# A two-layer graph network on one core: the setup, the first and the last pairs written out in an order of their own on each engine

## The reference

```python
# layer 0
h = relu(layernorm(x))
x = x + adj @ (h @ W0) + b0
# layer 1, 8 heads of 256 features
h = relu(layernorm(x))
f = (h @ fc_w + fc_b)                       # per head: feat_proj, 128 x 256
q, k = f @ q_w + q_b, f @ k_w + k_b
masked = leaky_relu(q + k^T + (1 - adj) * -1e9, 0.01)
attn = softmax(masked)
x = x + sigmoid(concat_heads(attn @ f) @ fp_w + fp_b + h)
```

## Time and profile before

| | |
|---|---|
| median of 3 runs | 1457.86 us (1457.38 to 1458.21) |
| profiled execution, its own time | 1458.05 us |
| its span (first to last instruction) | 1456.3 us |
| PE busy | 1437.4 us, 99% |
| DVE busy | 1280.5 us, 88% |
| ACT busy | 1130.4 us, 78% |
| POOL busy | 1100.7 us, 76% |
| mean granted TensorE clock | 0.993 of 2.4 GHz |
| PE's share of the chain that ended last | 97% |

### The profile page before, as it was taken

How to read it: one execution, slowest core, us unless ns; L and a number is a source line. 1 busy time by engine, 2 the same in 40 slices (tenths; PEclk the granted TensorE clock), 3 DMA queues, 4 the chain that set the end, 5 groups by cost and what they waited for, 6 DMA issues and landing times.

```text
span 1456.3 us, 31565 instructions
## 1 busy us (share of the span) xinstructions
PE 1437.4 (99%) x9128; PEld 1286.0 (88%) x9128; DVE 1280.5 (88%) x4393; ACT 1130.4 (78%) x3477; POOL 1100.7 (76%) x1293
## 2 busy tenths in 40 slices
PE   7899999999999999999999999999999999999998
PEld 6788898898888888888988988888888988988887
DVE  5789889889889889889898898898898898898886
ACT  3677877877877878778778778778778778778776
POOL 3677777787787787787777877777777777877864
PEclk9899999999999999999999999999999999999999
DMA  5221221221221221221221221222212212212211
GB/s 191 88 103 69 87 103 60 93 102 53 100 102 52 101 102 52 101 102 52 101 94 59 101 87 67 101 79 73 102 69 84 102 59 94 102 52 101 73 47 42
DMA packets 42651, 123.88 MB, mean 85 GB/s; under 512 B 4224, under 2 KB 9216, under 8 KB 42624
## 3 DMA queue, kind: packets, MB, share of 16 engines
q1 hardware_dynamic: 42336, 123.55, 23.3%
q10 hardware_dynamic: 288, 0.01, 0.0%
HBM read 105.46 MB, written 18.09 MB: 85 GB/s over the span
## 4 chain that ended last, share of the span: by engine, by line
PE 97%; issue 1%; DMA 0%; DVE 0%; ACT 0%; POOL 0%; POOLq 0%; SPq 0%
PE gbank L272 49%; PE ybank L272 25%; PE tbank L388 8%; PE bank L272 6%; PE bank L339 4%; PE bank L367 2%; PE bank L357 2%; PE gbank L292 1%; PE bank L373 0%; DMA late<-fp_w_dram 0%; POOL att L900 0%; ACT att L750 0%; DVE kq_sb L568 0%; POOLq L44 0%; ACT h L719 0%
## 5 line engine op out<-in xcount | busy, mean ns | idle before, releaser
L893 POOL TENSOR_TENSOR att<-late,t_pos 128x512 f32<-128x512 f32 x256 | 331.1, 1294 | 135.3 <-PE tbank L388 134.2
L272 PE MATMUL gbank<-m_hi,hT_lo 128*128 128x512 f32 x1024 | 431.4, 421 | 0.0
L750 ACT ACTIVATE att<-att 128x128 f32<-128x128 f32 x1024 | 397.9, 393 | 39.8 <-DVE att L601 34.8
L272 PE MATMUL gbank<-m_hi,hT_hi 128*128 128x512 f32 x1024 | 406.1, 397 | 0.0
L272 PE MATMUL gbank<-m_lo,hT_hi 128*128 128x512 f32 x1024 | 405.7, 396 | 0.0
L577 DVE TENSOR_TENSOR g_lo<-gbank,g_hi 128x512 fp32r<-128x512 f32 x512 | 342.5, 680 | 48.0 <-ACT g_hi L743 43.1
L900 POOL TENSOR_TENSOR att<-att,rinv 128x512 f32<-128x512 f32 x256 | 289.9, 1132 | 112.4 <-DVE rinv L606 112.2
L743 ACT ACTIVATE g_hi<-gbank 128x512 fp32r<-128x512 f32 x512 | 289.9, 594 | 59.0 <-PE gbank L272 58.9
L594 DVE TENSOR_SCALAR_CACHE_REDUCE att<-att,qs 128x128 f32<-128x128 f32 x1024 | 291.9, 342 | 37.5 <-POOL att L893 37.5
L272 PE MATMUL ybank<-g_hi,pT_lo 128*128 128x256 f32 x1024 | 293.8, 287 | 0.0
L272 PE MATMUL ybank<-g_hi,pT_hi 128*128 128x256 f32 x1024 | 289.7, 283 | 0.0
(11 more groups left out here) (87 smaller groups left out, 2359.0 us busy)
## 6 DMA issues: line engine op xcount, KB each, us to landing
late<-key_rows SPq DMA_DIRECT2D x64, 1024.0 KB, 5.9
g_in<-graph_dram SPq DMA_DIRECT2D x64, 512.0 KB, 3.3
out_dram<-res SPq DMA_DIRECT2D x64, 256.0 KB, 3.2
late<-fp_w_dram SPq DMA_DIRECT2D x4, 512.0 KB, 9.2
key_rows<-kq_sb SPq DMA_DIRECT2D x64, 20.0 KB
att<-fc_wT_dram SPq DMA_DIRECT2D x2, 512.0 KB, 6.5
late<-fc_wT_dram SPq DMA_DIRECT2D x2, 512.0 KB, 9.9
w_f<-w_dram SPq DMA_DIRECT2D x1, 256.0 KB, 8.3
```

What stands on the lines that cost most here:

```text
L272: mm = pe.matmul(out_ap, w, m, start=first and n == 0, stop=last and n == len(terms) - 1)
L750: e = act.activation(a[:, s], a[:, s], ACT.Exp, scale=-1.0, bias=a[:, CH + h:CH + h + 1], accum_out=esum[j][c][:, h:h + 1])
L893: gp.tensor_tensor(a, keys[q][:, j, c * HC:(c + 1) * HC, :], t_pos[q][:, j, :].unsqueeze(1).broadcast_to([P, HC, P]), ALU.add)\
```

## The change

Nothing is computed in another way. Steps 4 to 60 of PE (and the like stretches of the other engines) keep their loop and its order. `setup` and the steps ahead of the loop become one list for each engine (`begin`), and those behind it another (`finish`), each with calls from several pairs mixed in a new order. The main points:

- The weights come in five pieces, of 1, 1, 2, 2 and 2 heads, so the first two are 0.5 MB. `load` of pair 1 is issued ahead of piece 2 and that of pair 2 ahead of piece 4. The small loads have a semaphore each instead of a shared one.
- `warm` has 10 products instead of 18.
- Pair 1's `aggregate` and `transform` stand among or right behind the folds, pair 2's and 3's between pair 0's projections; seven projections of pair 0 stand ahead of its first `transpose_p` (four before).
- `keys_queries` of pair 1 stands on DVE ahead of pair 0's `mask_min`.
- `transpose_h` waits also for `v_hTlo` of the pair before, in the loop too.
- In the last pairs the calls of `step` stand in a slightly different order.

The core of the diff (in `finish` of PE the calls go on in this manner down to `attend(63, 1, 1)`):

```diff
+WARM = 10
+
+PIECES = ((0, 1), (1, 2), (2, 4), (4, 6), (6, 8))
+STARTS = [h for h, _ in PIECES]
...
+            def weights_in(c):
+                t = slice(DT * PIECES[c][0], DT * PIECES[c][1])
+                at = slice(t.start % H, t.start % H + t.stop - t.start)
+                sp.dma_start(fcT_sb[t.start // H][:, at, :], fc_wT[:, t, :]).then_inc(s_weights[c], 16)
...
+            def begin():
+                load(0, 0)
+                weights_out(0)
+                weights_in(0)
+                weights_out(1)
+                weights_in(1)
+                load(1, 1)
+                weights_in(2)
+                weights_out(2)
+                load_w0()
+                load_bias0()
+                weights_in(3)
+                load_identity()
+                weights_out(3)
+                load_key_bias()
+                load(2, 2)
+                load_output_bias()
+                weights_in(4)
+                weights_out(4)
+                load_query_bias()
+                load(3, 0)
+                load(4, 1)
+                keys_out(0, 0)
+                keys_in(0, 0)
+                keys_out(1, 1)
...
 
                 h, dt = n // DT, n % DT
-                if n % 4 == 0:
-                    pe.wait_ge(s_weights[n // 4], 32)
+                if dt == 0 and h in STARTS:
+                    pe.wait_ge(s_weights[STARTS.index(h)], 32)
...
                 if has(p - 1):
                     pe.wait_ge(a_qs, p)
+                    pe.wait_ge(v_hTlo, p)
+                else:
+                    pe.wait_ge(s_ident, 16)
...
+            def begin():
+                warm()
+                fold(0)
+                fold(1)
+                fold(2)
+                aggregate(0, 0)
+                key_query_bias()
+                fold(3)
+                fold(4)
+                fold(5)
+                fold(6)
+                transform(0, 0)
+                fold(7)
+                fold(8)
+                aggregate(1, 1)
+                fold(9)
+                fold(10)
+                fold(11)
+                fold(12)
+                fold(13)
+                fold(14)
+                fold(15)
+                transpose_h(0, 0)
+                transform(1, 1)
+                h_ready(0)
+                queries_keys(0, 0)
+                project(0, 0, 1)
+                turn_queries(0, 0)
+                aggregate(2, 2)
+                project(0, 0, 2)
+                transform(2, 2)
+                transpose_h(1, 1)
+                project(0, 0, 3)
+                h_ready(1)
+                queries_keys(1, 1)
+                project(0, 0, 0)
+                turn_queries(1, 1)
+                aggregate(3, 0)
+                project(0, 0, 4)
+                project(0, 0, 6)
+                project(0, 0, 5)
+                transpose_h(2, 2)
+                output_bias()
+                transform(3, 0)
+                transpose_p(0, 0, 0)
+                project(0, 0, 7)
+                transpose_p(0, 0, 1)
+                attend(0, 0, 0)
+                h_ready(2)
+                queries_keys(2, 2)
+                transpose_p(0, 1, 0)
+                attend(0, 0, 1)
+                project(1, 1, 1)
+                turn_queries(2, 2)
+                transpose_p(0, 1, 1)
+                attend(0, 1, 0)
+                project(1, 1, 2)
+                attend(0, 1, 1)
...
+            def finish():
+                h_ready(60)
+                project(60, 0, 7)
+                attend(60, 0, 1)
+                transpose_h(62, 2)
+                h_ready(61)
+                project(61, 1, 1)
+                attend(60, 1, 0)
+                project(61, 1, 2)
+                transpose_p(60, 1, 1)
+                h_ready(62)
+                queries_keys(62, 2)
+                project(61, 1, 3)
...
+            begin()
+            steady(pe, step, 4, 61)
+            finish()
...
+                fold_low(15)
+                u_low()
+                hT_low(0, 0)
+                residual0(1, 1)
+                key_query_bias()
+                bias_part(13)
+                keys_queries(0, 0)
+                bias_part(14)
+                bias_part(15)
+                stats1(1, 1)
...
+                keys_queries(1, 1)
+                mask_min(0, 0, 0, 1)
+                mask_min(0, 0, 0, 0)
+                leaky(0, 0, 1)
+                leaky(0, 0, 0)
+                g_low(0, 0)
+                ah_rest(3, 0)
+                mask_min(0, 0, 1, 1)
+                inverse(0, 0, 0)
+                mask_min(0, 0, 1, 0)
+                inverse(0, 0, 1)
+                leaky(0, 1, 1)
+                leaky(0, 1, 0)
+                output_row()
+                pT_low(0, 0, 0)
+                g_low(0, 5)
+                hT_low(2, 2)
+                inverse(0, 1, 0)
+                pT_low(0, 0, 1)
+                mask_min(1, 1, 0, 0)
+                g_low(0, 4)
+                inverse(0, 1, 1)
+                leaky(1, 0, 0)
+                keys_queries(2, 2)
+                pT_low(0, 1, 0)
+                g_low(0, 7)
+                g_low(0, 6)
+                mask_min(1, 1, 0, 1)
+                pT_low(0, 1, 1)
...
+            def begin():
+                load_bias()
+                load_key_query()
+                h0_relu(0, 0)
+                fold_high(0)
+                fold_high(1)
+                u_none()
+                fold_high(2)
+                ah_high(0, 0)
+                w0_high()
+                fold_high(3)
...
+                hT_high(0, 0)
+                u_high()
+                h0_relu(2, 2)
+                kq_rows(0)
...
+                exp(0, 0, 0)
+                exp(0, 0, 1)
+                hT_high(2, 2)
+                g_high(0, 5)
+                pT_high(0, 0, 0)
+                exp(0, 1, 0)
+                pT_high(0, 0, 1)
+                g_high(0, 6)
+                exp(0, 1, 1)
+                kq_rows(2)
+                g_high(0, 7)
+                pT_high(0, 1, 0)
...
+                mask_keys(0, 0, 0, 1)
+                variance1(2, 2)
+                mask_keys(0, 0, 0, 0)
+                rstd1(2, 2)
+                minus_mean1(2, 2)
+                shift1(2, 2)
+                mask_keys(0, 0, 1, 1)
+                mask_keys(0, 0, 1, 0)
+                normalise(0, 0, 0)
...
```

More of the change, by code:

```diff
@@ L173, in u_of, with steady @@
             return m[:, dt, :, D:D + 2].rearrange("p h k -> p k h").bitcast(F32)
[L175 to L180, removed]
+        def steady(eng, step, first, last):
             with eng.Fori(first, last - U + 1, U) as i:
@@ L250, in keys_in @@
                   .then_inc(s_keys, 16)
-            def step(i, q):
[L253 to L263, removed]
+            def begin():
[23 more added lines that the diff above has]
+                keys_out(1, 1)
+                keys_in(1, 1)
+                keys_out(2, 2)
+                keys_in(2, 2)
+                load(5, 2)
+                load(6, 0)
+                store(0)
+                keys_out(3, 0)
+                keys_in(3, 0)
+                keys_out(4, 1)
+                store(1)
+                load(7, 1)
+                keys_in(4, 1)
+                store(2)
+                keys_out(5, 2)
+                load(8, 2)
@@ L303, in output_bias @@
                 pe.matmul(ybank[:, 0:D], ones[:], c_part[:], start=True, stop=True).then_inc(pe_crow, 1)
[L305 to L320, removed]
-                pe.wait_ge(a_uhi, DT)
-                pe.wait_ge(v_ulo, DT)
-                h_ready(0)
-                queries_keys(0, 0)
-                output_bias()
             def ring_free(n, p):
@@ L344, in transform @@
                 pe.wait_ge(v_ah, p + 1)
+                if not has(p - 1):
+                    pe.wait_ge(v_w0lo, 1)
                 for j in range(J):
@@ L363, in queries_keys @@
             def queries_keys(p, q):
+                if not has(p - 1):
+                    pe.wait_ge(a_uhi, DT)
+                    pe.wait_ge(v_ulo, DT)
                 for dt in range(DT):
@@ new lines, in step @@
+            def step(i, q):
+                project(i - 1, (q + 2) % U, 7)
+                attend(i - 1, 0, 1)
+                transpose_h(i + 1, (q + 1) % U)
+                project(i, q, 1)
+                transpose_p(i - 1, 1, 1)
+                project(i, q, 2)
+                h_ready(i + 1)
+                queries_keys(i + 1, (q + 1) % U)
+                project(i, q, 3)
+                attend(i - 1, 1, 0)
+                project(i, q, 0)
+                turn_queries(i + 1, (q + 1) % U)
+                attend(i - 1, 1, 1)
+                transpose_p(i, 0, 0)
+                project(i, q, 4)
+                project(i, q, 6)
+                transform(i + 2, (q + 2) % U)
+                transpose_p(i, 0, 1)
+                project(i, q, 5)
+                attend(i, 0, 0)
+                aggregate(i + 3, q)
+                transpose_p(i, 1, 0)
```

(2 more changed lines are left out.)

1088 lines of the change are left out of this document (836 added, 252 removed).

## The result

The changed kernel takes 1445.17 us (median of 4 runs, 1444.14 to 1445.98); the kernel before, run beside it, 1457.98 (4 runs, 1457.38 to 1458.21). The ratio is 0.9914, with a 95% interval of 0.9902 to 0.9926. That is 12.8 us less, where 12.5 was forecast. The profiled execution is the fastest of the four, 1444.14 with a span of 1442.3, so the spans differ by 14.0.

The account below looks back on a forecast made before the run. PE was taken as the bound, busy 1437.4 of 1456.3 us, with nearly all winnable time before 51 us. A gain of 13.0 less 0.5 took 1458.05 to 1445.5, median 1445.3; range 1441.2 to 1450.5.

Parts of the forecast that it names:

- 5 to 7 that I had named as a sign: Opening on PE: waits after the first fold would total 5 to 7 us if the forecast was right.
- The start: Until the first fold: 7.2 instead of 8.29 us with a 0.5 MB first piece; warm products end at 6.3.
- Up to kq(0): Folds until queries_keys(0) starts on PE: 19.1 us of work from 7.2 plus 0.4 hand-overs, start at 26.7.
- Key rows to the first `transpose_p`: keys_out(0) issued at 28.8, write landing 3.2, broadcast 5.9, then 9.6 from masks: first transpose_p at 47.5.
- Down to `attend(0, 1, 1)`: After the first transpose_p: 13.7 us plus 0.8 for groups of a new kind; reached at 62.0, before 75.0, gain 13.0.
- my 0.5 for later waits: Pairs 1 to 3: 0.5 us taken off the gain of 13.0 for small waits not followed, leaving 12.5.
- The clock: Opening on PE after the first fold: half clock costs about 5.4 us, with waits 16.9.
- Rival 1: Opening: clock falls in the new waits, around 45 us; gain 9.5, time 1448.3; chance 0.22.
- Rival 2: Opening: folds come late, through weights or a clock not released, costing 2 to 3.5 us; time 1448; chance 0.12.
- Rival 3: Opening: nearly all comes back, key rows land in 2 us, 2 us of waits remain; gain 16, 1441.9; chance 0.12.
- Rival 4: Pairs 1 to 4: waits reappear since DVE has no slack; gain within 2.9 us, time about 1457; chance 0.03.
- rival 5: Added transpose_h wait stops PE 63 times; 0.2 us each eats the gain, 0.25 gives 1461; chance 0.02.

Follow-up runs that it names:

- `keys_queries(1)` back: Changed kernel with DVE's keys_queries(1) moved back behind pair 0's first two mask_min and leaky; 1449.33 us, ratio 0.9945.
- the four pieces: Changed kernel with the weights in four equal pieces of two heads instead of five pieces; 1446.38 us, ratio 0.9920.
- the third set: Last four experiments, on another chip: changed kernel unedited 1444.86 us, without added wait 1445.58, one warm product 1445.76, two waits shortened by reordering 1444.18.
- the first two sets: First eight experiments, four per set, on a different chip from the last four; kernel before beside them 1458.02 and 1457.72 us.
- the run with two waits removed: Changed kernel with weights ahead of pair 1's inputs, plus aggregate(1) behind fold(10), h0_relu(1) behind fold_high(8), pT_low ahead of output_row; 1444.18 us.

## Why the prediction was right, step by step

The forecast of 12.5 us met 12.8. The mechanism was as described: clock at 1.00, the long waits gone (4.0 us stayed, fewer than the 5 to 7 that I had named as a sign), loop and end unchanged, the added wait free, nothing given back behind. That the old order of the last pairs changes nothing shows that the gain lies in the opening. Several terms were mis-sized, and their errors cancelled.

- **The start.** I had the first fold at 7.2; it came at 5.91. The warm products end at 4.97, not 6.3, since their pace doubled some 2 us earlier than in the kernel before. POOL's copy starts at 5.49 instead of 7.09. It still waits for both small loads of ACT (these two share a semaphore after the change too, which the description above leaves out); but `fcb`, now asked for first, lands 3.9 us after its issue, where as the second it took 5.8. I had called that a mere change of places. With both limits gone the weights were last again. The step was worth 2.4 us at the fold, not 1.1; with a first piece of 1 MB the fold starts at 7.97, so 2.1 of it is the smaller piece.
- **Up to kq(0).** Forecast 26.7, measured 28.16, later than the 27.93 of before although the first fold came earlier. This is the step that failed, and for two reasons, of which either would have been enough. I had added up PE and DVE and left out POOL: behind the bias row, which lands at 13.2, POOL has the inputs of pairs 0, 1 and 2 ahead of `rstd1(0)`, which starts at 23.72, and that path alone gives 28.16. And the folds were held 1.33 us at `fold(4)` by the weights, which I had expected of a later piece, and not as likely. Without POOL, PE's own path would have come to about 27.6 (an estimate: 28.16 less the 0.22 us at kq(0) and the 0.3 at `aggregate(1)`). So taking `inputs(2)` off POOL's path gained only 0.2 us.
- **Key rows to the first `transpose_p`.** Three errors: the issue 1.2 us late (30.01, not 28.8), the way to the masks 6.6 instead of 9.1 us (2.5 less: 1.9 of the write's landing and 0.6 of the broadcast), and from the masks to `transpose_p` 10.9 instead of 9.6 (1.3 more). Together they make 0, and 47.49 for 47.5 proves nothing of the parts. The last one is DVE, which is full there, and the pace of its work is enough to account for it. Timeline of DVE:

```profile
41.05 2.92 DVE L800 SCALAR_TENSOR_TENSOR att<-att 128x516 f32<-128x516 f32 x2
```

  The first two `leaky` take 1.22 and 1.78 us, beside POOL's `mask_keys` (40.42 to 43.42 above). In the loop the median of one is 0.68, so they are 1.6 us longer, more than the 1.3 that was missing.
- **Down to `attend(0, 1, 1)`.** 13.74 us for the forecast 14.5. The 0.8 that I added for groups of a new kind was not there. The point came at 61.23 against 62.0, 13.8 us ahead of the 75.0 of before, and the spans differ by 14.0: my 0.5 for later waits was not lost either. That my sum of the parts met 13.74 to 0.1 us may be luck, since its pieces were not measured one by one. That the medians give only 12.8 is because the profiled execution is the fastest of four.
- **The clock.** I priced it at 5.4 us; keeping the kernel before warm won 2.6 (3.7 if counted from kq(0) in the profiles). The total held all the same. By the profiles, the 13.8 us are 2.4 of an earlier start, 7.5 of fewer waits (11.5 to 4.0), and 3.9 left for the clock, the pace of folds and smaller things, of which that experiment shows 2.6 to 3.7. My sum had a larger clock and a smaller start, and again the two offset each other.
- **Rival 1** did not happen in the changed kernel. It did in the two runs that brought back a long wait: behind the 4.33 us of `keys_queries(1)` back the clock reads 0.60 from 45 to 46 us and 0.50 from 46 to 48, and in the 3.00 us of the four pieces it fell to 0.50. **Rival 2**, late folds, happened in small: 1.33 us for a piece of weights, and in the profiles of the third set three folds at near half pace. **Rival 3** asked for 2 us of waits; 4.0 stayed. **Rival 4** is refuted by the full stretches and the span, **rival 5** by the run without the wait.

What stays open: which parts make up the step from 3.5 us (pair 1's first part moved alone) and 2.6 (clock alone) to 12.8. The runs show only that `keys_queries(1)` ahead is worth 4.2 and the split first piece something near 1.2, each with all the rest in place; both sizes include a clock that fell. These are not shares that can be added.

## What to carry to other kernels

Where a steady loop is full, find the one point in the opening behind which the rest of the span is constant, and follow every engine's queue and the loads to it, the least busy engine too. Here two paths met there, about half a microsecond apart: POOL's queue (28.16) and PE's folds behind the weights (about 27.6, by the estimate above). The chain names only the one that ended last, and taking it away gains only the distance to the next. A slow stretch is not worth the excess of its durations, since part of it lies beside work that would be waited for anyway; and a wait removed alone comes back at the next link, so that one part moved alone won 3.5 us where work of several pairs moved together won 12.8. When a forecast hits, its intermediate points must be compared as well: here three errors of 1.2 to 2.5 us cancelled.

## What the runs showed of the hardware

- **The pace of the first products varies at a clock of 1.00 in the records.** Twelve fold products took 2.94 us in one profile of the changed kernel and 4.90 in another. In the other variants of the changed kernel in the first two sets they took 2.78 to 3.30 (the four pieces apart), in the four profiles of the third set, on the other chip, 4.86 to 5.53; whether that goes with the chip or with the run stays open. The granted clock of 6 to 11 us reads 1.00 in the slow case too:

```profile
6.00:11.00 5.00, 4.86 (x14) 3.94 (x15) 3.25 (x9) 1.95 (x5) 1.17 (x3) 1.00 1.00 331
```

  Fourteen products in 4.86 us, against 26 (ten of them short) in 4.93 in the first profile. The warm products of both kernels do the same: about 0.27 us from one to the next at first and half of that later, at a clock column of 1.00. The 4.34 us of the four pieces is another case, since the column reads 0.50 there. So ahead of the first fall of the clock the column doesn't show the pace; the mean duration of a product does.
- **A small write to memory lands fast.** Of the 20 KB of key rows of pair 0, the read that waits for the write is issued 1.34 us after the write, and 1.31 to 1.34 in all eleven profiles with the new opening.
- **DVE and POOL hold each other up, and it depends on the instruction and on which begins first.** `w_lo` took 0.68 us where POOL had nothing long beside it (the run with two waits removed), 0.88 in the kernel before, beside POOL's `t_pos` (one input), and 1.53 in the changed one, where it begins 0.29 us behind POOL's `xb` (two inputs). One `c_part` took 1.37 us beside the next `xb`, where 0.47 is usual. In the run with `keys_queries(1)` back `w_lo` began 0.06 us ahead of `xb`: it took 0.69 us, and `xb` 1.76 instead of 1.27. Where a `c_part` ahead of `w_lo` is stretched in this way, `transform(0)` waits 0.58 to 0.59 us for `w_lo` (four profiles). Timeline of DVE in the changed kernel:

```profile
13.59 1.53 DVE L707 TENSOR_TENSOR w_lo<-w_f,w_hi 128x512 fp32r<-128x512 f32 x1 [0.34 <-ACT w_hi L1146]
...
16.77 0.47 DVE L682 SCALAR_TENSOR_TENSOR c_part<-late,fcb,c_part 128x256 f32<-128x256 f32 x1
...
17.77 1.37 DVE L682 SCALAR_TENSOR_TENSOR c_part<-late,fcb,c_part 128x256 f32<-128x256 f32 x1
```
